# q, k and v of one attention layer by Strassen's scheme: seven block products in place of eight

## What is computed

```python
h = relu(layernorm(x))
q, k, v = h @ Wq + bq, h @ Wk + bk, h @ Wv + bv          # heads of 64
weights = softmax(q k^T / 8 + mask(adj))
x = x + weights @ v
h = relu(layernorm(x))
q, k, v = h @ Wq1^T, h @ Wk1^T, h @ Wv1^T
rel = adj^T * (q k^T);  rel = rel / norm(rel, axis=2)
x = x + rel @ v
```

## Time and profile before

| | |
|---|---|
| median of 3 runs | 2421.3 us |
| the profiled execution | 2422.4 us |
| its span, first to last instruction | 2420.6 us |
| TensorE busy | 2391.3 us (99%) |
| ScalarE busy | 1686.1 us (70%) |
| VectorE busy | 1454.1 us (60%) |
| GpSimd busy | 1301.7 us (54%) |
| mean granted clock of TensorE | 0.999 of full speed |

### The profile page before, as it was taken

The page is one execution under the profiler, slowest core; times in us unless marked ns, Lnnn a source line. Parts: engine busy times, 40 slices in busy tenths (PEclk is TensorE's granted clock), DMA queues, the critical chain, the costliest instruction groups (busy, mean ns, idle before and its releaser), DMA issues.

```text
span 2420.6 us, 53556 instructions
## 1 busy us (share of the span) xinstructions
PE 2391.3 (99%) x19252; PEld 1299.4 (54%) x19252; DVE 1454.1 (60%) x4435; ACT 1686.1 (70%) x4111; POOL 1301.7 (54%) x1159
## 2 busy tenths in 40 slices
PE   8999999999999999999999999999999999999998
PEld 4455555555555555555555555555555555555554
DVE  5665666655666555665556665556655566655664
ACT  5867777667776677776777766777667777667773
POOL 3655555555555555555555555555555555555561
PEclk9999999999999999999999999999999999999999
DMA  7756676666677566776566765667755667656663
GB/s 206 148 123 125 136 152 140 135 129 130 133 153 140 115 131 133 153 141 128 128 131 144 149 137 121 132 132 153 143 127 127 132 146 149 131 124 135 134 125 70
DMA packets 938361, 328.09 MB, mean 136 GB/s; under 512 B 886000, under 2 KB 886256, under 8 KB 938096
## 3 DMA queue, kind: packets, MB, share of 16 engines
q1 hardware_dynamic: 935312, 319.43, 63.3%
q10 hardware_dynamic: 2784, 5.24, 0.6%
HBM read 72.88 MB, written 33.55 MB: 44 GB/s over the span
## 4 chain that ended last, share of the span: by engine, by line
PE 90%; DMA 2%; ACT 2%; DVE 2%; issue 1%; POOL 1%; DVEq 0%; SPq 0%; ACTq 0%
PE B L728 76%; PE S L804 7%; PE O L728 7%; DMA probs_t<-halves 2%; ACT probs L529 1%; DVE stats L592 0%; ACT h L473 0%; ACT halves L537 0%; DVE masked L665 0%; POOL v L423 0%; DVE rel_halves L699 0%; POOL halves L427 0%; ACT h_halves L480 0%; DVE result L706 0%; DVE v_sum L657 0%
## 5 line engine op out<-in xcount | busy, mean ns | idle before, releaser
L427 POOL TENSOR_TENSOR halves<-probs,halves 128x512 f16<-128x512 f32 x512 | 598.1, 1168 | 561.5 <-ACT halves L537 561.2
L529 ACT ACTIVATE probs<-masked,neg_max 128x256 f32<-128x256 f32 x1024 | 508.3, 498 | 204.4 <-DVE neg_max L665 204.2
L665 DVE CUSTOM_DVE_ANT_0 masked<-S,mask 128x256 f32<-128x256 f32 x1024 | 385.7, 415 | 129.8 <-PE S L804 125.5
L413 POOL TENSOR_TENSOR h_halves<-h,h_halves 128x512 f16<-128x512 f32 x256 | 295.3, 1159 | 155.7 <-ACT h_halves L480 155.7
L728 PE MATMUL B<-wv,h0t 128*128 128x512 f16 x1536 | 354.1, 380 | 3.9 <-DMA h0t<-h_halves 2.5
L728 PE MATMUL B<-h0t,wq 128*128 128x512 f16 x1536 | 352.8, 379 | 0.0
L728 PE MATMUL B<-h0t,wk 128*128 128x512 f16 x1536 | 352.5, 379 | 0.0
L728 PE MATMUL B<-h1t,wm 128*128 128x512 f16 x1488 | 336.5, 379 | 1.3 <-DMA h1t<-h_halves 1.3
L728 PE MATMUL B<-wvt,h1t 128*128 128x512 f16 x1488 | 336.7, 379 | 1.1 <-issue 1.1
L537 ACT ACTIVATE halves<-probs 128x512 f16<-128x512 f32 x512 | 322.6, 630 | 20.3 <-PE O L728 4.2
L728 PEld LDWEIGHTS O<-v,probs_t 128*128 128x128 f16 x6144 | 245.8, 98 | 126.1 <-DMA probs_t<-halves 9.9
(11 more groups left out here) (78 smaller groups left out, 2983.0 us busy)
## 6 DMA issues: line engine op xcount, KB each, us to landing
x_in<-in_x_dram SPq DMA_DIRECT2D x128, 256.0 KB, 3.1
out_dram<-result SPq DMA_DIRECT2D x128, 256.0 KB, 3.4
x_res<-in_x_dram SPq DMA_DIRECT2D x124, 256.0 KB, 3.3
probs_t<-halves SPq DMA_TRANSPOSE x512, 2.8
h0t<-h_halves SPq DMA_TRANSPOSE x132, 3.2
h1t<-h_halves SPq DMA_TRANSPOSE x124, 3.3
rq<-in_L_gnn_Wq_dram ACTq DMA_DIRECT2D x4, 256.0 KB, 4.9
x_res<-in_L_gnn_Wk_dram ACTq DMA_DIRECT2D x4, 256.0 KB, 5.4
```

Of the source, the lines that this page charges most:

```text
L413: nc.gpsimd.tensor_tensor(h_halves[:, n, 1, :], h[:, n % 2, :], h_halves[:, n, 0, :], ALU.subtract).then_inc(h_low[layer], 1)
L427: nc.gpsimd.tensor_tensor(halves[:, n % RING, 1, :], probs[:, n % 2, :, :].rearrange("p t n -> p (t n)"), halves[:, n % RING, 0, :], ALU.s ...
L529: ins = nc.scalar.activation(probs[:, n % 2, i, :], masked[:, n % 2, i, :], ACT.Exp, bias=neg_max[:, n % 2, i:i + 1], scale=-1.0, accum_ou ...
L665: ins = nc.vector.tensor_tensor_reduce(out=masked[:, n % 2, i, :], in0=S[n % 4][:, i, :], in1=mask[:, i, :], scale=SCORE, scalar=BIG, op0= ...
```

## The change

- **Seven products for eight.** The features and the rows of h are each cut in two, as are both sides of the weights, which gives 256 x 256 blocks. Eight block products become seven (Strassen's scheme in Winograd's form) for each of q, k and v. A block product is two times six matmuls of 256 columns into one bank.
- **Sums.** Four sums of h blocks are made in place in `x_in` on VectorE (`h_sum`), in float32, before they are split; `ln0_apply` writes to `x_in` too. Seven blocks of h are split and transposed instead of four tiles. The seven weight blocks are summed and split once at the start. The products are added up on VectorE in `u` and `whole`; a finished quarter gets its high half on ScalarE and its low half on GpSimd (`halves_q`, `halves_k`, `halves_v`).
- **Bias of v.** It is added to the residual rows (`biased`, VectorE) and no longer to v.
- **Buffers.** `h0t` has one buffer of seven blocks, `h_halves` three places, probs three buffers that also hold the masked scores (`SOFT`), `attn`, `rel` and `v` one.
- **Timetable.** All slots are new, and the tables of the first and last pairs hold the same numbers as the general one.

The diff, cut to its core ("..." marks what is left out):

```diff
+    SOFT = 3
...
+    PRODUCT_AT = {("q", 0): 0, ("q", 1): 1.3, ("q", 2): 1.6, ("q", 3): 2.5, ("q", 4): 3.5, ("q", 5): 4.5, ("q", 6): 5,
+                  ("k", 0): 5.5, ("k", 1): 5.55, ("k", 2): 5.85, ("k", 3): 6.75, ("k", 4): 7.25, ("k", 5): 8,
+                  ("k", 6): 8.5, ("v", 0): 11.25, ("v", 1): 11.55, ("v", 2): 12.35, ("v", 3): 13.75, ("v", 4): 14.5,
+                  ("v", 5): 15.75, ("v", 6): 16, ("rv", 0): 42.75, ("rv", 1): 43.5, ("rv", 2): 45.25,
+                  ("rv", 3): 45.75, ("rq", 0): 47.75, ("rq", 1): 48.5, ("rq", 2): 49, ("rq", 3): 51, ("rel", 0): 54,
+                  ("rel", 1): 56.75, ("out", 0): 61, ("out", 1): 62.5, ("out", 2): 66.75, ("out", 3): 67.25}
...
+    BLOCKS = 7
...
+    SPLIT_ORDER = (4, 0, 1, 2, 3, 5, 6)
+    APPLY_ORDER = (2, 3, 0, 1)
+    WHOLE = {1: (0, 0), 4: (1, 0), 5: (1, 1), 6: (0, 1)}
+    PART = {j: i for i, j in enumerate(WHOLE)}
...
+    SCORED = [8.75, 12.75, 20.0, 26.5]
+    MASKED = [9, 12, 16.25, 19, 23.0, 25.5, 29, 31]
+    MULTIPLIED = [14.25, 14.75, 16.5, 17, 21, 22.5, 23.75, 25, 27.75, 28.75, 29.75, 31, 34, 34, 35.25, 36]
+    LAYER0 = {"x_in": [-25, -24.75, -24.5, -24], "ln0_stats": [-14.75, -12.75, -12.5, -9.75], "ln0_power": [-9.75],
+              "ln0_scale": [-9.5], "ln0_apply": [-8.5, -8.25, -7.5, -7.25], "ln0_sum": [-7, -7, -6.5, -5.25],
+              "ln0_split": [-8, -7, -6.5, -4, -3.25, -2.25, 0], "x_res": [9.5, 13.75, 15.25, 15.25],
+              "biased": [16.75, 19, 20, 20.5], "residual": [20.5, 25.5, 31.75, 35.5]}
+    LAYER1 = {"ln1_stats": [38, 38.25, 38.5, 38.5], "ln1_power": [38.75], "ln1_scale": [39.5],
+              "ln1_apply": [41, 41, 41.25, 41.5], "ln1_split": [41, 41.25, 41.5, 41.75], "squares": [55.75, 59.25],
+              "rel_scale": [56, 60], "rel_split": [57, 60.75]}
...
+    HALVES = 3
+    SPLITS = [("ln0_split", n, 0) for n in range(BLOCKS)]
+    SPLITS += [step for step in PLAN if step[0] == "ln1_split" or step[0] == "ln0_split" and step[2] > 0]
+    PLACE = {step: i % HALVES for i, step in enumerate(SPLITS)}
+    PLACE_BEFORE = dict(zip(SPLITS[HALVES:], SPLITS))
...
-        h_halves = sb("h_halves", [P, TILES, 2, D], fp16)
-        h0t = sb("h0t", [P, 2, 2, KT, TOK], fp16)
+        h_halves = sb("h_halves", [P, HALVES, 2, D], fp16)
+        h0t = sb("h0t", [P, BLOCKS, 2, 2, N], fp16)
+        u = sb("u", [P, 2, 2, N])
         q_st = sb("q_st", [P, KT, 2, TOK], fp16)
         k_st = sb("k_st", [P, KT, 2, TOK], fp16)
-        v_sum = sb("v_sum", [P, 2, D])
-        v = sb("v", [P, 2, 2, TILES, D], fp16)
+        whole = sb("whole", [P, 2, 2, N])
+        v = sb("v", [P, 2, TILES, D], fp16)
...
-        masked = sb("masked", [P, 2, NT, N])
-        neg_max = sb("neg_max", [P, 2, NT])
-        probs = sb("probs", [P, 2, NT, N])
+        probs = sb("probs", [P, SOFT, NT, N])
+        neg_max = sb("neg_max", [P, SOFT, NT])
...
+        def h_block(n):
+            return (quarter(x_in, 0, 0), quarter(x_in, 0, 1), quarter(x_in, 0, 0), quarter(x_in, 1, 0),
+                    quarter(x_in, 1, 1), quarter(x_in, 1, 1), quarter(x_in, 0, 1))[n]
...
-                    sp.wait_ge(ln_done[0], TILES * (p - 1) + n + 1)
+                    sp.wait_ge(h_low[0], BLOCKS * p)
...
-                    need(sp, p_product, NPC * (p - 1))
-                    turn_h(0, n, p)
+                    sp.wait_ge(p_product, P_COUNT["v", SPLIT_ORDER[n], p - 1])
+                    turn_h0(n, p)
...
+            def h0_low_half(n, pair):
+                step = ("ln0_split", n, pair)
+                pool.wait_ge(h_high[0], BLOCKS * pair + n + 1)
+                nc.gpsimd.tensor_tensor(halves_by_column(step, 1), by_column(h_block(SPLIT_ORDER[n])),
+                                        halves_by_column(step, 0),
+                                        ALU.subtract).then_inc(h_low[0], 1)
...
+                if kind in ("halves_q", "halves_k", "halves_v"):
+                    c = len(WHOLE) * projection(kind[-1], p) + n
+                    dst = projected(kind[-1], n)
+                    pool.wait_ge(whole_high, c + 1)
+                    nc.gpsimd.tensor_tensor(dst(1), whole[:, c % 2, :, :], dst(0), ALU.subtract).then_inc(whole_low, 1)
...
+                        pool.wait_ge(biased, TILES * (p + 1))
...
+            def h0_high_half(n, pair):
+                step, b = ("ln0_split", n, pair), SPLIT_ORDER[n]
+                if b in (0, 1, 4):
+                    act.wait_ge(ln_done[0], TILES * pair + (2 if b == 4 else TILES))
                 else:
+                    act.wait_ge(summed_blocks, 4 * pair + {5: 1, 3: 2, 2: 3, 6: 4}[b])
+                place_free(act, step)
+                nc.scalar.activation(halves_by_column(step, 0), by_column(h_block(b)),
+                                     ACT.Copy).then_inc(h_high[0], 1)
...
+            def weight_high(i, w, scale):
                 for part in range(2):
+                    act.wait_ge(w_part[i][part], 16)
+                act.wait_ge(w_sums, 4 * (i + 1))
+                for n in range(BLOCKS):
+                    nc.scalar.activation(w[:, n, 0, :, :], w_block(i, n), ACT.Copy, scale=scale).then_inc(w_high, 1)
+            for n in range(TILES):
+                ln0_apply(n, 0)
+            for n in range(BLOCKS):
+                h0_high_half(n, 0)
+            weight_high(0, wq, QS)
+            weight_high(1, wk, WS)
+            weight_high(2, wv, WS)
...
+                if kind in ("q", "k", "v") and n == 0:
+                    i = projection(kind, p)
                     act.wait_ge(p_product, P_COUNT[kind, n, p])
+                    need(act, whole_done, len(WHOLE) * i)
+                    nc.scalar.activation(u[:, 0, :, :].rearrange("p t n -> p (t n)"), B[BANK[kind, n, p]][:, :],
+                                         ACT.Copy).then_inc(u_first, 1)
+                elif kind in ("halves_q", "halves_k", "halves_v"):
+                    c = len(WHOLE) * projection(kind[-1], p) + n
+                    g, f = list(WHOLE.values())[n]
+                    act.wait_ge(whole_done, c + 1)
+                    if kind == "halves_v":
+                        need(act, summed, UNITS * (p - 1) + 8 * (f + 1))
+                    elif p > 0:
+                        act.wait_ge(scored, UNITS * (p - 1) + 8 * (f + 1))
+                    nc.scalar.activation(projected(kind[-1], n)(0), whole[:, c % 2, :, :],
+                                         ACT.Copy).then_inc(whole_high, 1)
...
+            def h_sum(n, pair):
+                a11, a12, a21, a22 = [quarter(x_in, i, j) for i in range(2) for j in range(2)]
+                low = BLOCKS * pair + 1
+                if n == 0:
+                    dve.wait_ge(h_low[0], low + SPLIT_ORDER.index(4))
+                    ins = nc.vector.tensor_tensor(a22, a21, a22, ALU.add)
+                elif n == 1:
+                    dve.wait_ge(ln_done[0], TILES * (pair + 1))
+                    dve.wait_ge(summed_blocks, 4 * pair + 1)
+                    ins = nc.vector.tensor_tensor(a21, a11, a21, ALU.subtract)
+                elif n == 2:
+                    dve.wait_ge(h_low[0], low + SPLIT_ORDER.index(0))
+                    dve.wait_ge(summed_blocks, 4 * pair + 2)
+                    ins = nc.vector.tensor_tensor(a11, a22, a11, ALU.subtract)
+                else:
+                    dve.wait_ge(h_low[0], low + SPLIT_ORDER.index(1))
+                    dve.wait_ge(summed_blocks, 4 * pair + 3)
+                    ins = nc.vector.tensor_tensor(a12, a12, a11, ALU.subtract)
+                ins.then_inc(summed_blocks, 1)
...
+            for n in range(4):
+                h_sum(n, 0)
+            for i, (w, scale) in enumerate(((wq, QS), (wk, WS), (wv, WS))):
+                b11, b12, b21, b22 = [quarter(stage[i], j, k) for j in range(2) for k in range(2)]
                 for part in range(2):
+                    dve.wait_ge(w_part[i][part], 16)
+                need(dve, w_low, BLOCKS * i)
+                nc.vector.tensor_tensor(whole[:, 1, :, :], b22, b12, ALU.subtract).then_inc(w_sums, 1)
+                dve.wait_ge(w_sums, 4 * i + 1)
+                nc.vector.tensor_tensor(b12, b12, b11, ALU.subtract).then_inc(w_sums, 1)
+                dve.wait_ge(w_sums, 4 * i + 2)
+                nc.vector.tensor_tensor(u[:, 1, :, :], b22, b12, ALU.subtract).then_inc(w_sums, 1)
+                dve.wait_ge(w_sums, 4 * i + 3)
+                nc.vector.tensor_tensor(whole[:, 0, :, :], b21, u[:, 1, :, :], ALU.subtract).then_inc(w_sums, 1)
+                for n in range(BLOCKS):
+                    dve.wait_ge(w_high, BLOCKS * i + n + 1)
+                    if n == 0:
+                        dve.wait_ge(w_sums, 4 * i + 4)
+                    nc.vector.scalar_tensor_tensor(w[:, n, 1, :, :], w_block(i, n), scale, w[:, n, 0, :, :],
...
+                if kind in ("q", "k", "v") and n > 0:
+                    i = projection(kind, p)
+                    product = B[BANK[kind, n, p]]
```

(54 more changed lines are left out.)

341 lines of the change are left out of this document (174 added, 167 removed), and 10 rows, old and new, of tables (PRODUCT_31, PRODUCT_AT).

## The result

The changed kernel takes 2620.3 us (median of 4 runs, 2612.6 to 2622.5) against 2421.6 us for the kernel before (4 runs): a ratio of 1.0815, interval 1.0793 to 1.0838. It is slower by 199 us. The forecast was 2485 with a range up to 2540: the sign is right, the size is 135 us short, and the time lies outside the range. The profiled execution took 2622.5 us around a span of 2620.7.

What follows compares the result with a forecast made beforehand. The prediction took TensorE as the bound before, then waits from a VectorE-GpSimd lock. Head 117, thirty pairs of 75.0 (2250), tail 117 and 0.7 outside the span gave 2485 us, 8-in-10 range 2375 to 2540.

Steps and rivals of the forecast that it cites:

- the walk: Written order followed: head's weight halves done at 51.3 us, tail's eight products and two rel from 74 to 102.
- C: Rival: lock also stops layer norm's chain step by step between power and shift; P 78.6, 2593 us; chance 0.10.
- P: Time of one steady pair, forecast 75.0 us: 70.5 of TensorE work plus waits of 0.9 and 3.6.
- the forecast's 3.6: Stretch behind rv: VectorE sums and bias taking turns with GpSimd start rq 1 3.6 us late; bounds 0 and 7.
- the chain into rv: From the last residual through layer norm and transposes to layer 1's rv product: rv waits 0.9 us; bounds 0 and 3.
- the products' term: TensorE's q, k and v as 21 block products: saves 3.6 us a pair, P 70.5 if nothing else makes it wait.
- rival A: TensorE stays the bound, queues miss each other and small waits hide: P 70.5 to 72.6, 2350 to 2413 us; chance 0.33.
- The head: Stretch before the second pair's scores: first scores about 68 us, then 49 to the second pair's.
- H: Start of the second pair's scores, forecast 117 us, bounds 112 and 124, against 88.1 before.
- The tail: Last pair's layer 1 runs alone under the common timetable, 117 us after its first scores; bounds 112 and 123.
- T: What follows the last pair's first scores, forecast 117 us, against 117.2 before.

Runs made afterwards that it cites:

- e1: Changed kernel with the four sums of h blocks and four bias additions replaced by equally long one-operand VectorE statistics instructions, computation left out: 2516.6 us.
- e6: Changed kernel with the refinement of the layer norm's power in three fused VectorE steps for four, everything computed: 2615.7 us.
- e4: Changed kernel with one-operand instructions for sums and biases, and one refine step for four in layer 0's norm, computation left out: 2444.3 us.
- e3: Changed kernel with one refine step in place of four in layer 0's norm, three left out of the computation: 2524.7 us.
- e2: Changed kernel with the sums of h blocks and bias additions on half the columns, still two SBUF operands, other half left out: 2555.7 us.
- e7: e6 with the four sums of x_in on GpSimd instead of VectorE, everything computed: 2509.6 us.
- e5: Kernel before, plain q, k and v, with one timetable for all pairs, special tables of first two and last three dropped: 2453.5 us.

## Why the prediction was right and wrong

**What held.** The 256-column products cost what was said: five blocks, sixty matmuls, step in 6.56 us (1385.69 to 1392.25), 1.31 each. The first scores stand at 68.4 for 68, in part by luck: by the walk's own rates the halves of the weights take 4.8, 7.8 and 7.8 us, and not 5.4, 8.4 and 8.4, and they ended at 50.8 for its 51.3. The sums of VectorE are stopped, all of them, with means of 1369 to 1648 ns; of the bias additions, mean 923, one in four is, not all as forecast. The stop happens beside GpSimd, and TensorE loses time at the second rq behind rv 2: place and mechanism are those of the forecast, and e1, where the same length of work that isn't stopped takes back 104 us, shows the cause. The forecast's wording of the condition, both operands in SBUF, fits the sums but not L699. The Trainium skill (SBUF — State Buffer, "SBUF: two separate sides") has this pair of ports as an exclusive lock held for a whole instruction; by that rule the trace agrees here for both sides (VectorE 1.65 us for 0.69, GpSimd 1.60 for 1.16). The sign, slower, is right.

**The step that failed most: C was priced, and left out of the sum.** The forecast had C's mechanism and its 3.6 us, gave it 0.10 "against: the trace shows one stopped step in a chain, not several", and summed with P = 75.0. (Its base is one pair's 74.1; over thirty pairs it is 73.8.) The measured P of 78.8 is near C's 78.6, in part by luck: C charged 7.2 us a pair to the lock and 0.9 to other waits, and the runs show 5.8 for the lock and 2.8 outside it. The argument against C was a misreading, and the trace of before could have shown it. Its rows of one layer norm, GpSimd and VectorE:

```profile
989.84 1.02 POOL L408 TENSOR_TENSOR guess<-var,half 128x4 f32<-128x4 f32 x1 [2.85 <-DVE var L602]
990.83 1.16 POOL L427 TENSOR_TENSOR halves<-probs,halves 128x512 f16<-128x512 f32 x1
...
991.00 1.01 DVE L580 TENSOR_TENSOR ln_work<-guess,var 128x4 f32<-128x4 f32 x1
992.04 0.16 DVE L582 TENSOR_TENSOR ln_work<-ln_work,guess 128x4 f32<-128x4 f32 x1
```

One step is stopped because one operation stood behind the power, and GpSimd was idle after it for 2.40 us. The trace showed a rule (one stop for each ready operation), and I took its instance (one) for the rule. The new order puts four operations there, which the forecast itself says ("four halves stand behind that power"). e6 is the run that pins this form of it down.

**The lock's size.** Measured in place of the forecast's 3.6: 5.8 us a pair (P of the changed kernel, 78.8, less that of e4, 73.0). The sums and biases alone give back 3.5 (e1), the chain alone 3.05 (e3), with the clock's part in both. 1.0 of the 5.8 is not waiting, but the clock, which no term had. In the changed kernel the block after the wait of 2.83 or 2.84 us is, in 15 of 25 pairs, slower than its own work:

```profile
1277.05 4.45 PE L908 MATMUL B<-h1t,wm 128*128 128x512 f16 x12 [2.84 <-DVE rv L859]
...
1277.00:1281.50 4.50, 4.45 (x18) 1.79 (x19) 4.50 (x13) 0.64 (x3) 3.83 (x3) 0.62 0.26 58
```

The second line is the table by stretches (length, PE, PEld, VectorE, ScalarE, GpSimd busy, granted clock, DMA share, GB/s): a granted clock of 0.62 is mostly 1.2 GHz in place of 2.4. In the pair shown at the top, after a wait of the same 2.84 us, the block took 2.76 and the clock was 1.00. Of the 25 such blocks between 300 and 2300 us, 15 take 4.05 to 5.30 us and ten 2.76: 24.7 us lost, 1.0 a pair. The mean of the group's matmuls is 404 ns. In e1, e2, e4 and e7, where no wait for rv passes 1.7 us, it is 379 and no block is slow; in e3, with waits of 2.0 to 2.65, 8 of 24 are. So a wait of 2.8 us costs up to 2.5 more than its length, and 1.0 in the mean.

**Without the lock the forecast was still 1.6 us short.** e4's P is 73.0 where the sum without the lock says 71.4. About half of it is waiting: 1.6 us a pair for u, for the transposed h1t and for rel, where the sum had 0.9. The h1t wait is what "the chain into rv" gave 0.9, and it is 0.6 in the changed kernel; u and rel, at 0.8 and 0.4, were nowhere. The other half is in the products' term, 70.5: TensorE is busy for 71.2 us a pair in e4 (1951.3 us in the 27.4 pairs), for 73.7 before (1996.9 in 27.1), which is 2.5 less and not 3.6. Single blocks do step in 1.31, so the loss lies between blocks; no run shows where. u and rel are evictions between neighbouring products. That blocks of 1.31 us in place of 2.59 bring TensorE back to a bank before the 0.69 us eviction behind its queue is done would explain them; no run separates this. e4's P lies above rival A's whole range, 70.5 to 72.6, so A would probably not have come true even without the lock.

**The head, 14 us.** "From first to second pair took 51 us; I keep 49" was taken from a pair with its own timetable. Without it the old kernel needs 60.1 (e5), which is 9 of the 14. The measured 62.9 has two things in it that the forecast's single line on the head did not have: 8.37 us at the third scores, where VectorE has the next layer norm's four stopped steps (86.64 to 91.08) ahead of the maximum, and a granted clock of 0.64 to 0.67 from 94 to 112 us after it. The lock is the smaller part of it: in e4, with two of the stops left, the wait is still 6.8, and H is 128.8.

**The tail, 8 us.** TensorE's last rows but three of the changed kernel's timeline:

```profile
2574.01 12.31 PE L908 MATMUL B<-wvt,h0t 128*128 128x512 f16 x48 [9.54 <-DMA h0t<-h_halves]
2586.16 10.52 PE L908 MATMUL B<-h0t,wm 128*128 128x512 f16 x48
...
2609.27 8.27 PE L908 MATMUL B<-rv,rel_t 128*128 128x512 f16 x24 [5.68 <-issue]
```

The products begin 78.0 us after the last scores, 4 later than walked. Behind the 9.54 us wait 48 matmuls take 12.31 us, and the 48 after them, of the same shape, 10.52; behind the 5.68 us wait 24 take 8.27, where 24 at 216 ns are 5.2. So 4 us are the walk's, and nearly 5 are a clock that falls in the gaps of a lonely tail and that no term had; the wait ahead of the outs was 5.7 us, shorter than the walk's 8 to 10. As the kernel before gains 15 us at this end by its tables (e5), a tail without one was the place for the upper bound, 123, and not for the middle.

**The break-even moves too.** With H and T as measured, the changed kernel would need P = (2421.3 - 0.7 - 131.25 - 124.7) / 30 = 72.2 to equal the kernel before; e4's 73.0 is above it. The saved products (3.6 us a pair, 108 us in all) were eaten in three places: 5.8 us a pair by the lock and what it does to the clock, some 2.8 outside the lock (1.6 in short waits that the old order did not have, the rest in products that saved 2.5 us and not 3.6), and 51 us at the two ends (43 and 8), where the common timetable alone cost the old kernel 25. 174 + 84 + 51 - 108 = 201, against 199 measured.
